# A paced gather: GpSimd clears a small tile behind every second gather of an edge stage and waits for it

## The reference, cut to what matters

```
feat_all = einsum('ni,rhid->rnhd', layernorm(x), conv_weights)
feat_src_e = feat_all[edge_type, edge_src]
e = leaky_relu(el + er); alpha = softmax of e over equal edge_dst
x = x + segment_sum(alpha * feat_src_e, edge_dst) + h_bias
x = x + sum over the top 2 experts of weight * ffn(layernorm(x))
```

## Time and profile before

| what | us |
|---|---|
| median of three timed runs | 2082.75 |
| lowest, highest | 2082.37, 2084.45 |
| the profiled execution, first to last instruction (its span) | 2456.4 |
| node stage, to the first gather | 243.6 |
| gathers, first to last start | 243.6 to 1806.6 |
| last gather to the end of the edge stage | 1806.6 to 1883.2 |
| route and expert stage | 1883.2 to 2456.3 |

### The profile page before, as it was taken

How to read it: one execution, slowest core, us unless ns; L and a number is a source line. 1 busy time by engine, 2 the same in 40 slices (tenths; PEclk the granted TensorE clock), 3 DMA queues, 4 the chain that set the end, 5 groups by cost and what they waited for, 6 DMA issues and landing times. The chain is left out here.

```text
span 2456.4 us, 35279 instructions
## 1 busy us (share of the span) xinstructions
PE 1898.8 (77%) x9138; PEld 1594.8 (65%) x9139; DVE 1062.3 (43%) x3018; ACT 1076.9 (44%) x3259; POOL 1142.0 (46%) x1164
## 2 busy tenths in 40 slices
PE   8999125767767777867777777677877689999998
PEld 7887124656655665656565666565665668999887
DVE  6332013545555555545555555455567532221111
ACT  2222123645555545554555555454656532222221
POOL 4000744556666566666666566656620443122222
PEclk9999556787877768777787777777788689999999
DMA  6443422333333333333333333333312877777774
GB/s 239 189 170 143 109 67 74 84 90 88 90 92 92 88 88 91 90 88 90 88 92 92 89 90 90 92 85 88 91 44 80 282 230 221 248 246 247 241 234 104
DMA packets 121157, 315.51 MB, mean 128 GB/s; under 512 B 27047, under 2 KB 71335, under 8 KB 106180
## 3 DMA queue, kind: packets, MB, share of 16 engines
q0 software_dynamic: 60192, 149.24, 23.4%
q1 hardware_dynamic: 60836, 164.88, 19.3%
HBM read 257.36 MB, written 57.71 MB: 128 GB/s over the span
## 5 line engine op out<-in xcount | busy, mean ns | idle before, releaser
L798 POOL DMA_INDIRECT gath<-feats,idxT x996 | 950.6, 954 | 799.1 <-issue 272.7
L1154 PE MATMUL psP<-gath,hot 128*128 128x260 f32 x1992 | 668.1, 493 | 28.6 <-DVE gath L905 15.1
L1154 PEld LDWEIGHTS psP<-gath,hot 128*128 128x128 f32 x1992 | 469.4, 247 | 123.5 <-issue 35.4
L1113 PE MATMUL psOT<-cst,hot 128*128 128x128 f32 x996 | 196.1, 331 | 346.0 <-ACT hotT L1045 231.9
L1045 ACT COPY hotT<-psOT 128x512 f32<-128x512 f32 x249 | 143.5, 576 | 628.6 <-remote 485.4
L1113 PEld LDWEIGHTS psOT<-cst,hot 128*128 128x128 f32 x996 | 139.7, 171 | 407.2 <-issue 309.0
L1138 PEld LDWEIGHTS psE<-er,hotT 128*128 128x128 f32 x1992 | 309.7, 235 | 48.6 <-issue 44.9
L914 DVE TENSOR_TENSOR acc<-acc,psP 128x260 f32 x498 | 211.0, 424 | 295.3 <-remote 127.9
L1138 PE MATMUL psE<-er,hotT 128*128 x1992 | 309.5, 305 | 31.1 <-issue 19.9
L1035 ACT ACTIVATE hot<-cst,ndlT 128x128 f32<-128x128 f32 x996 | 316.2, 391 | 4.7 <-PEq L325 4.7
L1680 ACT ACTIVATE acc<-psH,w1buf 128x256 f32<-128x256 f32 (+1 forms) x344 | 122.4, 423 | 346.7 <-PE psH L1571 304.3
(11 more groups left out here) (232 smaller groups left out, 1178.5 us busy)
## 6 DMA issues: line engine op xcount, KB each, us to landing
w1buf<-in_experts SPq DMA_DIRECT2D x43, 1030.0 KB
w2buf<-in_experts SPq DMA_DIRECT2D x43, 1024.0 KB
feats<-frow SPq DMA_DIRECT2D x29, 1040.0 KB, 3.9
gath<-feats,idxT POOLq DMA_INDIRECT x996
meta<-in_edges SPq DMA_DIRECT2D x464, 12.0 KB
acc<-slots_x SPq DMA_DIRECT2D x23, 258.0 KB
gath<-in_b SPq DMA_DIRECT2D x43, 128.0 KB
acc<-slots_x SPq DMA_DIRECT2D x20, 129.0 KB
```

Of the source, the lines that this page charges most:

```text
L798: pool.indirect_dma_start(gath[:, r, u], None, feats, bass.IndirectOffsetOnAxis(ap=idxT[:, r, u:u + 1], axis=0)).then_inc(gath_in[r], 16)
L1113: ins = pe.transpose(psOT[:, k * P:(k + 1) * P], hot[:, r, j * QUAD + k], ident)
L1154: ins = pe.matmul(psP[:, bank(g, b, r), 0:FW], hot[:, r, u], gath[:, r, u], start=u % BLK == 0, stop=u % BLK == BLK - 1)
```

## The change

Behind every second gather GpSimd clears a tile `pace` of 128 x 128 floats, which nobody reads, signals `paced`, and waits for that signal before it goes on. The wait's value counts pairs, so it is met only by this clear.

```
+        pace = t("pace", [P, P])
+        paced = sem("paced")
...
                         for u in range(j * QUAD, (j + 1) * QUAD):
                             pool.indirect_dma_start(gath[:, r, u], None, feats,
                                                     bass.IndirectOffsetOnAxis(ap=idxT[:, r, u:u + 1], axis=0)).then_inc(gath_in[r], 16)
+                            if u % 2:
+
+                                pool.memset(pace[:], 0.0).then_inc(paced, 1)
+                                wait_apart(pool, paced, pairs_before(g) + u // 2 + 1, carrier)
```

## The result

The changed kernel takes 2485.76 us (median of four runs, 2484.54 to 2487.26) against 2083.36 for the kernel before (2082.37 to 2084.45): 402 us more, a ratio of 1.193 with a 95% interval of 1.191 to 1.194. The forecast was 2525, in a range of 2270 to 2645. The profiled execution of the changed kernel took 2487.26 us in all, 1.9 us more than its span; so timed runs and trace now tell of the same thing. In the earlier trace rows they did not.

What follows compares the result with a forecast made beforehand. The prediction took GpSimd's uncovered chain of gathers as the bound. 2082.75 plus 438 for 498 pauses, plus 9 for loop jumps, minus 8 of tail gave 2522, said as 2525 us; range 2270 to 2645.

Steps and rivals of the forecast that it cites:

- The bound: GpSimd's chain of 996 gathers, 1.257 us apart without a pause, holds the timed kernel; sum 2105 us against 2082.75 measured.
- The cost of a pause: On GpSimd between a pair's second gather and the next gather: 0.88 us each, 438 us for 498.
- A slower first gather behind each clear: On GpSimd, the first gather after other work may take longer: 0 to 0.19 us, taken as 0.05.
- The dear end of a pause: Upper end of one clear and wait on GpSimd: 1.12 us, giving a forecast end of 2641 us.
- Loop jumps: At nine or so turns of GpSimd's loop, the jump back is no longer hidden: 1 us each, +9 us.
- The two kinds of time: Profiled span and timed median, 374 us apart before, end close together; the span grows only 86 us, to 2542.
- the patches: Mid-stage stretches of the first profile where all engines stand idle, about 10 us a period, perhaps only in profiled execution.
- Partly covered: Rival: other engines bound timed runs at 38.4 us a period, so GpSimd's pauses are partly hidden: 2275 us; chance 0.15.
- faster: Rival: idle stretches of all engines exist in timed runs and pauses break up gather bursts: 2003 us; chance 0.03.
- hidden: Rival: GpSimd's 10 us of slack a period holds in timed runs and swallows the clears: 2083 us; chance 0.04.
- dearer: Rival: task switch, start of clear and a longer next gather make each pause 1.3 us: 2730 us; chance 0.08.
- The rule on shared ports: VectorE's two-port operations block GpSimd's SBUF access; a clear might be held 0.22 us, under 4 us in all, not summed.

Runs made afterwards that it cites:

- 2: The kernel before without two of the 32 gathers in each of groups 4 to 30: 2017.92 us, ratio 0.967.
- 3: Every second gather of groups 4 to 30 left out: 1920.25 us on the kernel before, 1957.73 us on the changed kernel.
- 1: The kernel before, unedited, timed and profiled a second time: 2085.41 us, ratio 1.000, span 2087.2 us.
- before_again: The kernel before, unedited, in its second profiled execution (the run also called 1): 2085.41 us, ratio 1.000.

## Why the prediction was right, point by point

**The bound.** Right, and now shown: each gather is paid in full (2), the other engines could do 34.2 us a period (3), and an undisturbed profile has the period at 40.2 us (1). The prediction got there from a trace that said otherwise, by one check: if GpSimd never waits, first gather + 996 x 1.257 + tail + last stage is 2105 us, near the timed median, and the trace's own slack was about as large as the gap between its span and that median. The 22 us by which that sum was too high come from the disturbance as well: it took the last stage from the disturbed trace, 573.1 us, where it is 549.5. Its bounds of 32.6 to 38.4 us for the other engines' period held 34.2, as far as a kernel with half the gathers can tell.

**The cost of a pause.** Forecast 0.88 us, measured 0.82: the mean distance of gathers went from 1.2606 to (1906.0 - 244.8) / 995 = 1.6696 us, 407 us over 995 distances, shared by 498. Its parts: gather to clear nothing (0.10 was taken; this is one of the two terms that were mis-sized); the clear 0.221 (0.204); clear to next gather mostly 0.79 or 0.95, mean 0.87 (0.83, read off gathers that had waited for TensorE, another case of a GpSimd queue that has run dry); less 0.30. A slower first gather behind each clear (0.05 was taken) isn't there: the median record is 958 against 953 ns, 0.005 us. The two terms together are 498 x 0.145 = 72 us too much; clear and restart, a little dearer than taken, give 28 back, and a term that the forecast doesn't have gives some 12 more: in 13 pairs, 64 gathers apart, the gap between the first gather and the second is 1.10 us instead of 0.30 (and once 1.48). That leaves 438 - 72 + 28 + 12 = 406, against 407. So the forecast's nearness is in part errors of opposite sign.

**A slip in the range.** The dear end of a pause was worked out wrongly: with 0.30 and 0.19 the sum is 0.30 + 0.204 + 0.83 - 0.30 + 0.19 = 1.22 us, not 1.12, and its end of the forecast is 2082.75 + 608 + 1, some 2690 us and not 2641. The range, to 2645, therefore didn't hold the forecast's dear end as it says. The result, far below, isn't touched by it.

**The small terms.** Loop jumps were put at +9: in the changed kernel the gap at a loop head is longer by some 0.5 us (2.67 us between starts, against 2.13 at a quad), under 5 us in all. The tail behind the last gather's start is 579.4 us against 589.2 in `before_again`, 9.8 less where 8 was said. Sum: 2087.2 + 406.9 - 9.8 + 1.1 (a start 1.1 us later) = 2485.4, which is the span measured.

**The two kinds of time.** The span was to grow by about 86 us and the median by 442; they grew by 29 and 402, and they end together, as said. Of the 57 us by which the span stayed below the 2542 said, 23 are the last stage, which took 573.1 us only in the disturbed trace. But the prediction left open whether the patches belong to profiling as such or to one execution. It is the latter: each of the nine later profiles agrees with its timed runs within 0.2%.

**The signs.** Each that was named came: a pair of gathers every 2 x 1.6696 = 3.34 us (3.39 said), a period of 53.6 (54.3) set by landings, and hardly a wait for `psP`. The profile does put 51 gaps in front of gathers, 48.0 us in all, down to `psP`, but these are 0.94 us each in the mean and 1.2 at most, no longer than those put down to the clear in the same places.

**The rivals.** "Partly covered" is refuted by 2, "faster" by 1 (no patches in an undisturbed execution, so nothing for a pause to set free), "hidden" by the result, "dearer" by the clear's start at the gather's end and the unchanged record. The rule on shared ports, which the prediction took from the Trainium skill, "SBUF — State Buffer", section "Who interferes with whom", didn't come into it. The clears took 0.221 us in the mean against 0.204 of the one in the earlier trace rows, 8 us over all 498, but these aren't holds: the shortest of them took 0.218 and the longest 0.260, ten ran beside a conversion on VectorE, and none was held for the 0.22 us of one.

## What to carry to other kernels

When a profiled execution is much longer than the timed runs, find out which stage holds the difference before reading slack from it: here a trace with 10 us of idle time a period on GpSimd belonged to a kernel in which GpSimd had none, and its last stage was 23 us too long besides. A chain of like instructions on one queue gives a floor (count x distance) that can be set against the timed median by itself.

A wait on one's own just-issued instruction costs mostly the emptied queue: without it clears and waits were a tenth of the price (41 of 402 us), and what it adds is the longer restart behind the clear (0.87 us in the mean against 0.16). The instruction's own length is then paid as well, so a short one helps a little (56 us). If such a wait is needed, ask for an older one; and leave some run-ahead: with two gathers and a clear of it no gather started late, with one gather and a clear 22 did.

To make this kernel faster one would have to shorten or thin out GpSimd's gathers. Down to 34.2 us a period 164 us came back; whether the other engines keep that period with the full traffic of the gathers isn't shown.

## What was not expected of the hardware

Between two gathers there are 0.30 us, between a gather and a clear at most 0.01, and between a clear of 0.22 us that isn't waited for and a gather only 0.16 (0.19 behind one of 0.12). That part of a gather's preparation runs beside the clear would explain it; no run shows it apart. TensorE's granted clock was lower where it waited longer: 0.88 in the mean of a mid-stage period of the undisturbed kernel before, in which it was busy for 31.4 us of 40.2, and 0.78 in the changed one, busy for 32.6 of 53.5, though it does the same matmuls. The changed kernel's period is explained by the gathers alone, so nothing is left that the lower clock could have cost.
